# A square root, first loads, turns and a weight split at other units of the attention heads

## The reference

```
h = _layernorm(x) * (1 + ca) + sa
q = (h @ q_w.T + q_b).reshape(b, s, 16, 32); k = h @ k_w.T + k_b; v = h @ v_w.T + v_b
attn = softmax(where(causal, -inf, q @ k / 32 ** 0.5))
x = x + ga * ((attn @ v) @ o_w.T + o_b)
h = _layernorm(x) * (1 + cb) + sb
u = fwht(h * SU_ug) / 64
y = silu(u @ W_gate.T * (Wscale_gate * 64)) * (u @ W_up.T * (Wscale_up * 64))
x = x + gb * ((fwht(y * SU_dp) / 64) @ W_down.T * (Wscale_dp * 64))
```

## Time and profile before

| | |
|---|---|
| median of 3 runs | 2005.16 us (2001.11 to 2005.29) |
| profiled execution, its own time | 1998.95 us |
| its span | 1997.1 us, so 1.85 us lie around the span |
| mean granted TensorE clock | 0.991 |
| busy: PE, PEld, DVE | 1930.4, 1505.8, 1377.9 us |
| busy: ACT, POOL | 860.9, 245.0 us |

### The profile page before, as it was taken

How to read it: one execution, slowest core, us unless ns; L and a number is a source line. 1 busy time by engine, 2 the same in 40 slices (tenths; PEclk the granted TensorE clock), 3 DMA queues, 4 the chain that set the end, 5 groups by cost and what they waited for, 6 DMA issues and landing times.

```text
span 1997.1 us, 31329 instructions
## 1 busy us (share of the span) xinstructions
PE 1930.4 (97%) x10816; PEld 1505.8 (75%) x10816; DVE 1377.9 (69%) x3296; ACT 860.9 (43%) x1615; POOL 245.0 (12%) x589
## 2 busy tenths in 40 slices
PE   6999999999999999998999999999999999999998
PEld 3566666666666556556888789999999999999997
DVE  6787777777767556675466787677676776667755
ACT  3366555556556554465222443333333323333221
POOL 2121123211321112113010010010010100101000
PEclk8899999999999999999999999999999999999999
DMA  7443344333433455645436988779788797787884
GB/s 232 125 109 77 101 115 106 106 91 104 118 105 76 138 175 163 207 152 174 159 133 237 363 325 332 285 292 353 281 295 329 290 352 290 294 329 287 325 309 164
DMA packets 116309, 424.32 MB, mean 212 GB/s; under 512 B 28076, under 2 KB 33452, under 8 KB 101944
## 3 DMA queue, kind: packets, MB, share of 16 engines
q1 hardware_dynamic: 104488, 371.92, 55.5%
q10 hardware_dynamic: 11664, 50.40, 6.7%
HBM read 318.16 MB, written 61.10 MB: 190 GB/s over the span
## 4 chain that ended last, share of the span: by engine, by line
PE 46%; DVE 5%; ACT 2%; DMA 1%; issue 1%; SPq 0%; POOL 0%; DVEq 0%; ACTq 0%
PE banks L1786 22%; PE banks L1877 15%; PE banks L1656 7%; DVE ln_stats L1220 1%; PE banks L1752 1%; PE banks L1746 1%; DMA upgate_items_dram<-items_ring 1%; DVE x_normed L1232 0%; DVE y L1345 0%; DMA upgate_raw<-in_w_ug 0%; ACT silu_gate L880 0%; ACT y_split L865 0%; ACT L880 0%; ACT L886 0%; DVE out_sb L1417 0%
## 5 line engine op out<-in xcount | busy, mean ns | idle before, releaser
L1877 PE MATMUL banks<-d_ring,y_split 128*128 128x512 f32 x1536 | 377.5, 392 | 1.9 <-DVE y_split L1365 1.9
L973 ACT ACTIVATE probs<-banks 128x512 f32<-128x512 f32 x576 | 312.6, 601 | 55.3 <-PE banks L1923 51.8
L1877 PEld LDWEIGHTS banks<-d_ring,y_split 128*128 128x128 f32 x1536 | 281.7, 188 | 56.9 <-DVE y_split L1365 2.1
L1786 PE MATMUL banks<-h_t_split,items_ring 128*128 128x256 f32 x2280 | 321.1, 283 | 1.9 <-DVE both L1322 1.9
L1786 PEld LDWEIGHTS banks<-h_t_split,items_ring 128*128 128x128 f32 x2280 | 298.9, 191 | 14.0 <-ACT h_t L791 4.0
L1946 PE MATMUL banks<-probs,v_ones 128*64 128x512 f32 (+3 forms) x1536 | 278.4, 497 | 3.0 <-POOL probs L1083 3.0
L1710 PE MATMUL banks<-k_stack,q_stacks 96*128 96x512 f32 (+3 forms) x768 | 251.8, 372 | 12.4 <-DMA q_stacks<-q_split 3.1
L1923 PE MATMUL banks<-q_stacks,k_stack 98*128 98x512 f32 (+3 forms) x768 | 251.1, 369 | 6.4 <-ACT probs L973 4.4
L1946 PEld LDWEIGHTS banks<-probs,v_ones 128*64 128x64 f32 x1536 | 118.4, 137 | 162.3 <-issue 132.4
L1786 PE MATMUL banks<-input_sums,items_ring 128*128 128x256 f32 x1710 | 236.2, 283 | 0.0
L1083 POOL TENSOR_SCALAR_AFFINE_SELECT probs<-probs 128x128 f32<-128x128 f32 x512 | 145.7, 308 | 671.2 <-ACT probs L973 671.2
(11 more groups left out here) (179 smaller groups left out, 2278.9 us busy)
## 6 DMA issues: line engine op xcount, KB each, us to landing
items_ring<-upgate_items_dram SPq DMA_DIRECT2D x94, 1792.0 KB, 7.3
d_ring<-down_split_dram SPq DMA_DIRECT2D x128, 512.0 KB, 8.1
q_stacks<-q_split SPq DMA_DIRECT2D x192, 128.0 KB, 2.5
o_group<-o_raw SPq DMA_DIRECT2D x128, 128.0 KB, 2.4
upgate_raw<-in_w_ug SPq DMA_DIRECT2D x32, 512.0 KB, 4.2
upgate_items_dram<-items_ring ACTq DMA_DIRECT2D x8, 1792.0 KB, 7.3
upgate_items_dram<-items_made ACTq DMA_DIRECT2D x8, 1792.0 KB, 6.6
x<-in_x SPq DMA_DIRECT2D x32, 256.0 KB, 3.2
```

Of the source, the lines that this page charges most:

```text
L973: nc.scalar.activation(pr[:, u, :], score_bank[:, at % SLOTS_SCORE, :], ACT.Exp, scale=SCALE).then_inc(exped, 1)
L1786: last = nc.tensor.matmul(item_bank(g, item), weights[:, a, item, k * P:(k + 1) * P], by_key(item_input(blk, item, m))[:, k, :], start=(k ...
L1877: last = nc.tensor.matmul(acc[:, t, :], ys[s][:, a, t * P:(t + 1) * P], dr[g % D_RING][:, m, :], start=(f == 0 and a + m == 0), stop=(f == ...
```

## The change

Five edits, all on the order of work in heads 45 to 63. (1) The matrix `across` gets memory of its own (the tile that was `spare`), its wait on `kst_ready` goes, and the first four loads of the folding stand one behind each of units 4, 5, 6 and 7 of head 45 instead of all behind unit 8. (2) `deviations(0)` stands right behind the last exponential of head 58, ahead of the folding's copy and the evacuation. (3) Turns 1, 2 and 3 go from units 2, 4, 6 of head 61 to units 4, 6, 8. (4) The second butterfly stage is called at unit 4 instead of 3 of head 62. (5) In head 63 the cast of the first up and gate weights goes from unit 5 to 2 and their split from unit 7 to 4.

```diff
-TURNS, HADS = [(4, 6), (3, 2), (3, 4), (3, 6)], [(1, 1), (1, 3), (1, 5), (1, 7)]
+TURNS, HADS = [(4, 6), (3, 4), (3, 6), (3, 8)], [(1, 1), (1, 3), (1, 5), (1, 7)]
-STORE_AFTER, LOAD_BEFORE = 1, 1
+STORE_AFTER, LOAD_BEFORE, FIRST_LOADS = 1, 1, 4
-                ob=place(s, "output_bias", [P, D]), ones=place(s, "spare", [P, P]),
+                ob=place(s, "output_bias", [P, D]), across=place(s, "across", [P, P]),
-            place(s, "under_across", [P, 2 * KT * P])
-            W["across"] = place(s, "across", [P, P])
+            W["across"] = A["across"]
                     if i == 0:
-                        act.wait_ge(kst_ready, 2 * B)
                         act.dma_start(across[:], io["across"]).then_inc(across_in, 16)
-                        if i == 0 and (ALL - left) * NU == H * NU + u + LOAD_BEFORE:
+                        if kind == "across" and i < FOLD_RING and (ALL - H, u) == (FOLDS[0][1] + 1, FIRST_LOADS + i):
+                            load_fold(kind, i)
+                        if kind == "along" and i == 0 and (ALL - left) * NU == H * NU + u + LOAD_BEFORE:
                             for first in range(FOLD_RING):
                                 load_fold(kind, first)
                     nc.scalar.activation(pr[:, u, :], score_bank[:, at % SLOTS_SCORE, :], ACT.Exp, scale=SCALE).then_inc(exped, 1)
+                    if (ALL - H, u) == (STAT_LEFT, NU - 1):
+                        deviations(0)
                     side_step(ends[u])
...
-                    if (left, u) == (STAT_LEFT, NU - 1):
-                        deviations(0)
-                    if (left, u) == (CAST_LEFT, 5):
+                    if (left, u) == (CAST_LEFT, 2):
                         cast_upgate(0)
...
-                    if left == CROSS_LEFT and u in (1, 3):
-                        cross(0, u // 2)
+                    if left == CROSS_LEFT and u in (1, 4):
+                        cross(0, u // 3)
-                    if (left, u) == (CAST_LEFT, 7):
+                    if (left, u) == (CAST_LEFT, 4):
                         split_upgate(0)
```

## The result

The changed kernel took 1992.76 us, the median of five runs (1992.08 to 1994.86). The kernel before took 2001.15 us in five runs (2001.11 to 2005.29), of which three are those that the forecast started from. The medians lie 8.4 us apart, which is a ratio of 0.9958; the ratio on record, formed over the runs, is 0.9948 (10 us), 95% interval 0.9935 to 0.996. The changed kernel is faster by either. The profiled execution of the changed kernel took 1992.76 us with a span of 1990.9 us; a span of 1990.5 had been forecast.

What follows compares the result with a forecast made beforehand. TensorE, busy 97% of the span, bounds the kernel, so only its pauses and low clock can be won. 2.9 + 1.6 + 0.8 + 0 + 1.3 = 6.6 us off 2005.16 gives 1998.6 us, range 1995.0 to 2003.0.

Steps and rivals of the forecast that it cites:

- the clock term: Head 46, at 662 us: without the pause the clock stays up, saving one fall of 3.4 us, worth 1.7 us.
- none of the edits touches what differs there, so I take the difference as it is: Whole kernel: the 6.2 us between profiled execution and median of the runs was carried over unchanged.
- Edit 1, pause 1.16 us: Head 46: TensorE's scores no longer wait 1.16 us for a late exponential; the spread load issues cost nothing.
- Edit 2, 1.6 us: Head 59: TensorE's pause shrinks from 2.24 to about 0.6 us; the folding's copy comes 0.1 to 0.3 us later, absorbed.
- Edit 3, 0.78 us: Head 61, unit 2: without a turn ahead of the maxima's copy, TensorE's pause of 0.78 us goes.
- Edit 4, nothing: Head 62: VectorE's order stays the same, so no gain and the 1.24 us pause stays.
- Edit 5, 1.3 us: Head 63: masks 0.94 us shorter and last exponential about 0.35 us earlier; exponentials of units 3 to 5 come 0.95 us later.
- It survives whole: Behind head 63: the chain to TensorE's weight wait has fixed lengths, load 7.40 us, so it moves as a whole.
- The clock does not pay: Head 46, rival: the fall at 662 us stays or comes at another pause; 2000.3 us (0.16), one more 2002.0 (0.08).
- ScalarE bounds head 63: Head 63, rival: TensorE waits for exponentials 0.95 us late, leaving a gain of 0.35 us; 1999.5 us, chance 0.10.
- The slower case: Heads 59 and 62, rival: clock falls at remaining pauses cost 1.7 us each; seven give 2010.5 us, chance 0.04.
- The table load: Head 59: by the trace 1.28 us without drain; by the skill's rule, 1.38 us drain besides and 1.4 us more gain.

Runs made afterwards that it cites:

- Edit 3 alone: Kernel before with only turns 1, 2 and 3 moved to units 4, 6 and 8 of head 61: 2000.73 us, ratio 0.9989.
- The real form of edit 4: Kernel of the early weights, plus VectorE's second butterfly stage waiting for GpSimd's masks of units 0 to 2 of head 62: 1989.87 us, ratio 0.9934 to before.
- the early weights: Changed kernel with a feed-forward step's up and gate weights issued by SyncE ahead of spreading the softmax sums: 1988.82 us, ratio 0.9934 to before.
- the kernel with the loads moved: Changed kernel with the matrix and all four first folding loads issued together behind unit 4 of head 45: 1993.28 us, ratio 0.9959 to before.
- the slower kernels: Changed kernel with two square root and exponential pairs added behind the last exponentials of four or eight heads: 2011.80 and 2029.41 us.
- four short delays: Changed kernel with a one-column square root and exponential added behind the last exponential of heads 22, 26, 36 and 40: 1993.87 us, ratio 0.9957 to before.

## Why the prediction missed

**The step that failed is the clock term**, in two sentences of the prediction. Edit 1 was given 1.7 us for "another 1.7 us lost", one fall at one place, and the sum then ended with "none of the edits touches what differs there, so I take the difference as it is". Both took the falls of one profiled execution for those of the kernel. Other executions of before have falls behind other pauses too: the profiled one had an L of 18.7 us, the mean of 73 is 24.3. The edits do touch this difference. The changed kernel's profile, with 18.8 us, lies near its mean of 18.3. By the split, the change took 1976.8 - 1972.6 = 4.2 us of F and 24.3 - 18.3 = 6.0 us of L (means over the 73 executions of before and ten of the changed kernel), 10.2 us together. The forecast had 4.8 us of pauses and 1.7 of clock. 6.0 / 1.7 is worth 3.5 falls fewer in each execution, not one. The rest of the miss is the starting point: the median of before was 2005.16 in three runs, 2001.15 in five, and 2003.25, 2002.93, 2003.44 and 2001.20 later. By an estimate from these numbers, of the 5.8 us by which the forecast time is off, 3.6 are the gain (10.2 against 6.6, all of it clock) and some 2.2 the three runs (2005.16 against 1976.8 + 24.3 + 1.85 = 2003.0).

Point by point:

- *Edit 1, pause 1.16 us:* right (gone; 1.1 us in F alone). The clock term of 1.7 us: too small, 3.5 ± 1.7 us in L alone. The issues cost nothing, as said; but it was the place, not the spreading.
- *Edit 2, 1.6 us:* right, 2.24 - 0.63 = 1.61 in the traces. The copy behind it did not come late at all: it starts 1.51 us behind the start of TensorE's matmuls for it in both traces (857.57 to 859.08 before, 854.51 to 856.02 now), and the evacuation is idle 1.24 us ahead in both. The 0.1 to 0.3 us of the prediction were not there.
- *Edit 3, 0.78 us:* right for the pause. Not foreseen: another 0.44 us in head 62. Edit 3 alone brings it, by butterflies that start 0.11 us behind the first of the five masks and not 0.56, and masks of 5.30 us and not 5.74. The prediction had the butterflies start later by the turn in unit 8; measured against the masks they start earlier. That the overlap sets the masks' length is read from the order in time, not tested by itself.
- *Edit 4, nothing:* right for VectorE's order. "The pause of 1.24 us of head 62 as it was" was wrong, by edit 3. The real form of edit 4, on top of the early weights, moves the pause to ScalarE's wait.
- *Edit 5, 1.3 us:* 1.79 - 0.23 = 1.56, inside its bounds; the exponentials of units 3 to 5 held nobody up.
- *It survives whole:* as far as the runs can tell (4.2 us in F). "Fixed lengths" was wrong, since the same weight load takes 7.40 or 7.86 us in the kernel before; a loss by the change is not shown. The one fall of the profile after stands behind that wait.
- *The rivals.* "The clock does not pay" had it the wrong way round: the clock paid at least as much as the pauses (6.0 against 4.2 us). It was right that a fall can come at another pause, but its evidence, no fall behind the pause of 2.24 us, was one draw. "ScalarE bounds head 63" did not come. The slower case (falls at the pauses that stay) has its mechanism, but fewer pauses bring fewer falls.

That the forecast span of 1990.5 us was met by 1990.9 is in part luck. The forecast had no fall left in it, but the execution had drawn one, at 939; without it the span would be 1.7 us shorter.

In all 15 profiles together there are 39 falls between the first 100 us and TensorE's last matmul, and every one begins within 5 us of the start of a pause of TensorE of about a microsecond or more (the shortest 0.99 us). The converse does not hold: before has twelve pauses of 0.97 us or more there and one or five falls, and the kernel with the loads moved has eight and none. What decides between them stays open.

Nor is it shown that each removed pause took only its own falls along. A pause of 1.07 us at 832 us or, in the slower kernels, up to 868, which no edit touches, brought a fall in 4 of the 6 profiles without edit 1 and in 2 of the 9 with it. If that is more than chance, a part of the 3.5 us of edit 1 was won at a pause that stayed. And alone the four edits that do something have 8.6 us in L, where the whole change has 6.0; the intervals allow that they simply add up.

The table load stayed as the earlier trace rows had it. In the changed kernel the root starts 0.02 us behind its load (854.19 + 1.28 against 855.49). By the Trainium skill (ScalarE: Activation LUTs, What ACT_TABLE_LOAD costs) a drain of 1.38 us would come on top; the trace shows none, neither here nor between the exponential ahead (it ends at 854.17) and the load, and the measurement decides.

## What to carry to other kernels

In this kernel, where TensorE is busy 97% of the time, pauses that were added or removed cost their own length and, on average, about as much again in clock: 9.4 us of added pauses cost 11.9 us of clock, 18.3 cost 20.5, and 4.2 us taken away gave back 6.0. Do not price them by the falls that one profiled execution shows. It is no rate for every pause either. The changed kernel keeps eight pauses of 0.97 us or more behind the first 100 us, 11 us together, and its L of 18.3 lies only 1 to 2 us above the 16.4 and 17.1 us of the two profiles that have no fall (loads moved, and four short delays). Before had twelve, 17 us together, and lay some 7 us above them. These are estimates from the profiles and the means of L. Split spans of many executions by their mean clock before you believe that a profiled execution stands for the median.

## What had not been expected of the hardware

- Executions of one kernel differ by falls of the clock that cost 1.7 us each: two profiles of before had one and five of them, with spans of 1997.1 and 2003.2 us.
- Two table loads with two one-column activations behind a last exponential, about 3 us of ScalarE, were mostly hidden in the middle heads: four of them brought two new pauses of 1.3 and 0.9 us. At head 59 the same kind of work had stopped TensorE for 2.24 us.
- GpSimd's mask of 0.29 us takes about 1.3 us beside a VectorE operation with two inputs: five masks took 5.30 us beside two butterfly stages and 3.31 beside one. The Trainium skill (SBUF — State Buffer, SBUF: two separate sides) gives a lock on a shared pair of ports as the cause, which a VectorE operation with two inputs in SBUF holds for its whole length against a GpSimd operation that reads SBUF; the traces agree with that, and no run here separates it from other causes.
